# Attention weighing in half steps, values and identity products moved into the lead, and a later output store, in a two-layer transformer kernel on one core

## The reference

```python
x = norm(x + state_space(x))          # first layer: a scan, then a mixture of experts
x = norm(x + experts(x))              # top 2 of 8
x = norm(x + attention(x))            # second layer: 16 heads of 16 features
x = norm(x + ffn(x))                  # gate/up/down, inputs and weights rounded to FP4

def attention(z):                     # per sequence; this is where the change lies
    zn = norm(z) * ln_w + ln_b
    q, k, v = split(zn @ W_qkv + b_qkv)            # 16 heads of 16
    a = softmax(q @ k.T / 4)                       # 1024 x 1024 for each head
    return z + concat(a @ v) @ W_proj + b_proj
```

## Time and profile before

| | |
|---|---|
| median of 3 runs | 1861.14 us (1858.03 to 1862.63) |
| the profiled execution | 1861.33 us, span 1859.8 us |
| mean granted TensorE clock | 0.907 |
| PE busy | 1623.9 us (87%) |
| DVE busy | 1275.1 us (69%) |
| ACT busy | 829.0 us (45%) |
| POOL busy | 245.7 us (13%) |

### The profile page before, as it was taken

One profiled execution on the slowest core, in us unless ns is written; L12 is line 12 of the kernel. 1 busy time (PEld: TensorE's weight loads), 2 busy tenths in 40 slices (PEclk: granted clock), 3 DMA queues, 4 the chain that ended last, 5 costly groups with the idle time before them and its releaser, 6 DMA issues.

```text
span 1859.8 us, 25712 instructions
## 1 busy us (share of the span) xinstructions
PE 1623.9 (87%) x7834; PEld 926.9 (50%) x7834; DVE 1275.1 (69%) x2551; ACT 829.0 (45%) x1255; POOL 245.7 (13%) x243
## 2 busy tenths in 40 slices
PE   5969999993899996989999788899986988999786
PEld 2748888882433324654333356433334653333354
DVE  3672222202589977858999687779968958997586
ACT  1302332230357773242776624257772333777421
POOL 0243222213000302010012030100303010000020
PEclk8989999997779998995999989779998986999898
DMA  3227777673412300022231000412300031210000
GB/s 127 68 70 233 259 224 231 226 219 110 68 19 36 86 2 1 1 51 42 36 71 35 1 1 2 92 18 36 87 2 1 1 65 30 40 31 1 1 1 23
DMA packets 80185, 123.06 MB, mean 66 GB/s; under 512 B 13529, under 2 KB 55770, under 8 KB 80042
## 3 DMA queue, kind: packets, MB, share of 16 engines
q1 hardware_dynamic: 71050, 94.25, 19.5%
q0 software_dynamic: 8992, 27.01, 4.9%
HBM read 76.84 MB, written 18.61 MB: 51 GB/s over the span
## 4 chain that ended last, share of the span: by engine, by line
PE 69%; DVE 19%; issue 6%; ACT 3%; POOL 1%; DMA 1%; SPq 0%; DVEq 0%; ACTq 0%; POOLq 0%
PE PS L953 12%; PE PS L998 12%; DVE MX L1449 10%; PE PS L870 7%; PE PS L882 7%; PE PS L1082 7%; PE PS L1092 5%; PE PS L927 3%; PE PS L985 3%; PE PS L939 2%; PE PS L821 1%; ACT Pb L691 1%; PE PS L1043 1%; PE PS L1112 1%; PE PS L860 1%
## 5 line engine op out<-in xcount | busy, mean ns | idle before, releaser
L1449 DVE TENSOR_REDUCE MX<-PS 128x1 f32<-128x512 f32 x1024 | 635.3, 682 | 84.0 <-PE PS L953 84.0
L691 ACT ACTIVATE Pb<-PS 128x1024 f32<-128x1024 f32 x512 | 499.7, 1023 | 253.1 <-PE PS L985 252.1
L953 PE MATMUL PS<-Ks,Qs 48*128 48x512 f32 x1024 | 404.9, 502 | 36.6 <-DVE MX L1449 14.2
L953 PEld LDWEIGHTS PS<-Ks,Qs 48*128 48x128 f32 x1024 | 181.7, 203 | 370.7 <-DVE MX L1449 352.6
L985 PE MATMUL PS<-Qs,Ks 50*128 50x512 f32 x1024 | 311.2, 460 | 5.9 <-ACT Pb L691 4.7
L998 PE MATMUL PS<-Pb,V 128*32 128x512 f32 x2048 | 290.2, 640 | 2.7 <-ACT Pb L691 2.7
L985 PEld LDWEIGHTS PS<-Qs,Ks 50*128 50x128 f32 x1024 | 145.5, 198 | 57.4 <-ACT Pb L691 52.4
L1350 DVE TENSOR_TENSOR V<-PS,V 128x512 f32<-128x512 f32 x39 | 27.0, 692 | 203.3 <-PE PS L882 203.3
L882 PE MATMUL PS<-Pb,OT 128*128 128x256 f32 x624 | 141.0, 379 | 0.0
L614 ACT ACTIVATE OT<-PS,b1t 128x256 f32<-128x256 f32 x156 | 65.5, 471 | 158.9 <-PE PS L870 158.9
L882 PEld LDWEIGHTS PS<-Pb,OT 128*128 128x128 f32 x624 | 115.7, 190 | 14.2
(11 more groups left out here) (278 smaller groups left out, 1834.6 us busy)
## 6 DMA issues: line engine op xcount, KB each, us to landing
Pb<-W SPq DMA_DIRECT2D x78, 512.0 KB, 4.0
y_slot<-V SPq DMA_DIRECT2D x39, 256.0 KB, 4.0
Qs<-Qh SPq DMA_DIRECT2D x128, 64.0 KB, 2.3
Ks<-Kh SPq DMA_DIRECT2D x128, 64.0 KB, 2.3
V<-b SPq DMA_DIRECT2D x39, 128.0 KB, 3.7
XT<-x_mid POOLq DMA_DIRECT2D x4, 1024.0 KB, 6.2
out<-X POOLq DMA_DIRECT2D x4, 1024.0 KB, 6.6
OT<-xT SPq DMA_DIRECT2D x2, 1024.0 KB, 6.4
```

What stands on the lines that cost most here:

```text
L691: F["ex"].inc(act.activation(Pb[:, kt % 2, 2 * qh:2 * qh + 2, :], PS[:, 2 * qh:2 * qh + 2, :], ACT.Exp, scale=0.25))
L953: F["slp"].inc(pe.matmul(PS[:, slot_bank(i), :], Qs[rows, p % NB, t * P:(t + 1) * P], Ks[rows, p % NB, kh * HALF:(kh + 1) * HALF], start=T ...
L1449: F["sld"].inc(dve.tensor_reduce(MX[:, p % 2, a, t, kh:kh + 1], PS[:, slot_bank(i), :], AX.X, ALU.max))
```

## The change

It has these parts:

1. **Weighing in halves.** W is split by query halves. Half qh waits only for the exponentials of half qh and writes 256 columns of bank 7 in each column group. The order of query tiles in the stack changes to match. A step is now S, T, S, W twice. `pv` counts halves, and ScalarE waits for the half it overwrites. The copy of bank 7 comes after the first exponential of a pair's first step, not after the second.
2. **Values and identity products in the lead.** `EARLY` is 2. Three S follow, then for each further value up to five S. `keep_warm` adds products of the identity with itself, whose result nobody reads: 8 after the first pair's last S, 3 after the next S, and one after each of the next five.
3. **Late last turn.** The turn of pair 7's maxima moves from right behind the last S to step 53, after its second T.
4. **Output in its own buffer.** The last norm writes `OB` (a part of `Pb`). Pool copies the next residual into `X` when the FFN's last sum is done, and stores `OB` once the first stack has landed. It sets the ones of `V` after that store.
5. **Stack of K shared with Pool.** Three of the twelve DMAs of the first stack (keys of head 1) are issued by Pool.
6. **Loop edge.** The rounding of QK unit 2 (ScalarE) and the low parts of units 0 and 1 (VectorE) move ahead of the loop edge.

```diff
@@ SP: stack(p) @@
-                        for a in range(2):
+                        for a in range(1 if p == 0 and dst is Ks else 2):
@@ Pool @@
-            def sequence(b, more):
-                F["xw"].wait(pool, b, TT)
+            def residual(b, ahead):
+                F["xw"].wait(pool, b, TT, ahead)
                 hold(pool, "pool")
                 F["xn"].inc(pool.tensor_copy(X[:, :, :], XN))
-                F["xn"].wait(pool, b, 1)
+            def first_keys(b, ahead):
+                F["qkv"].wait(pool, b, 4, ahead)
+                hold(pool, "pool")
+                for row, part in enumerate((Kh[DH:2 * DH, 0, :].bitcast(F32), Kh[DH:2 * DH, 0, :].bitcast(F32), Kl[0][DH:2 * DH, :].bitcast(F32))):
+                    at = ROW + row * DH
+                    F["kst"].inc(pool.dma_start(Ks[at:at + DH, 0, :].bitcast(F32), part), by=16)
+            def value_ones(b, ahead):
+                F["xn"].wait(pool, b, 1, ahead)
                 hold(pool, "pool")
                 F["vm"].inc(pool.memset(V[:, :, :, DH:32], 1.0))
...
+                if more:
+                    F["dr"].wait(pool, b, TT)
+                    residual(b, 1)
+                    first_keys(b, 1)
+                    F["stk0"].wait(pool, b, STK - KST, 1)
                 F["xa"].wait(pool, b, TT - 2 + TT // 2)
                 F["xd"].wait(pool, b, 2 + TT // 2)
-                F["outd"].inc(pool.dma_start(out..., X[:, :, :]), by=16)
+                F["outd"].inc(pool.dma_start(out..., OB), by=16)
                 F["outd"].wait(pool, b, 16)
+                if more:
+                    value_ones(b, 1)
@@ ScalarE @@
-                    F["pv"].wait(act, b, KT * (p + 1))
+                    F["pv"].wait(act, b, 2 * KT * (p + 1))
...
-                                F["pv"].wait(act, b, (n - 4) // 2 + 1)
+                                F["pv"].wait(act, b, n - 3)
...
-                        if kt == 0 and p > 0:
-                            evac_o(p - 1)
+                            if kt == 0 and p > 0 and qh == 0:
+                                evac_o(p - 1)
@@ TensorE @@
-                    for a in range(2):
+                    for a in (1, 0):
...
-                def weigh(m):
+                def weigh(m, qh):
                     p, kt = m // KT, m % KT
                     if kt == 0 and p:
                         F["ov"].wait(pe, b, p)
-                    F["ex"].wait(pe, b, 2 * m + 2)
-                    for qh in range(2):
+                    F["ex"].wait(pe, b, 2 * m + qh + 1)
+                    for c in range(2):
                         for a in range(2):
-                            j = 2 * a + qh
-                            ins = pe.matmul(PS[32 * j:32 * j + 32, 7, :], V[:, kt, 2 * p + a, :], Pb[:, kt % 2, 2 * qh + a, :],
-                                            start=(kt == 0), stop=(kt == KT - 1), skip_group_check=True)
+                            j = 2 * a + c
+                            ins = pe.matmul(PS[32 * j:32 * j + 32, 7, qh * QW:(qh + 1) * QW], V[:, kt, 2 * p + a, :],
+                                            Pb[:, kt % 2, 2 * qh + a, c * QW:(c + 1) * QW],
+                                            start=(kt == 0 and qh == 0), stop=(kt == KT - 1), skip_group_check=True)
                     F["pv"].inc(ins)
+                def keep_warm(n):
+                    for _ in range(n):
+                        pe.matmul(PS[:, 3, 0:P], ident[:, :], ident[:, :], start=True, stop=True)

                 for t in range(EARLY):
                     values(t)
-                F["vv"].wait(pe, b, EARLY - 1)
+                F["vv"].wait(pe, b, 1)
+                maxima(3)
                 F["qkv"].wait(pe, b, 8)
                 for t in range(EARLY, TT):
-                    maxima(8 * (t - EARLY + 1))
+                    maxima(5 * (t - EARLY + 1))
                     values(t)
                 F["vv"].wait(pe, b, TT)
                 F["vm"].wait(pe, b, 1)
-                maxima(UN + START)
+                maxima(UN)
+                keep_warm(8)
+                maxima(UN + SOON)
+                keep_warm(3)
+                for n in range(SOON, START):
+                    maxima(UN + n + 1)
+                    keep_warm(1)
+                LAST = (NP * UN - UN - LEAD) // 4
...
-                    transposed_scores(p, kt, 0)
-                    maxima(ahead + 2)
-                    transposed_scores(p, kt, 1)
-                    maxima(ahead + 3)
-                    if m:
-                        weigh(m - 1)
-                    maxima(ahead + step)
-                weigh(NP * KT - 1)
+                    for qh in range(2):
+                        maxima(ahead + 2 * qh + 1)
+                        transposed_scores(p, kt, qh)
+                        if qh and m == LAST:
+                            turn_max(NP - 1)
+                        maxima(ahead + (step if qh else 2))
+                        if m:
+                            weigh(m - 1, qh)
+                for qh in range(2):
+                    weigh(NP * KT - 1, qh)
```

More of the change, by code:

```diff
@@ L20 @@
 HALF = 512
+QW = HALF // 2
 NH = S // HALF
@@ L32 @@
 LEAD, START = 12, 6
-EARLY = 5
+EARLY = 2
 SOON, LATER = 1, 4
@@ L225, in transformer @@
         XQ = Pf[0]
+        OB = XQ.rearrange("p (t d) -> p t d", t=TT)
         XW = Pf[1][:, TT * D // 2:]
@@ L262, in transformer @@
             ve=1, rs=2, nm=1, vel=2, rsl=4, nml=2, zn=TT, xn=1, xw=TT, xa=TT - 2 + TT // 2, xd=2 + TT // 2, x2=1, vm=1, trp=4 + 2, xt=4 + 2, xl=TT - 3,
-            qkp=8, qka=8, qkv=8, vp=TT, vv=TT, **{f"stk{k}": NP // NB * STK for k in range(NB)}, mrow=16 * 2 * NP,
+            qkp=8, qka=8, qkv=8, vp=TT, vv=TT, **{f"stk{k}": NP // NB * STK - (0 if k else KST) for k in range(NB)}, kst=KST, mrow=16 * 2 * NP,
             slp=SLOTS, sld=SLOTS, nms=NP,
-            bp=2 * KT * NP, ex=2 * KT * NP, pv=KT * NP, ov=NP,
+            bp=2 * KT * NP, ex=2 * KT * NP, pv=2 * KT * NP, ov=NP,
             op=TT // 2, on=TT, mp=TT, mt=TT, pr=TT, rr=TT,
@@ L548, in _ @@
             gathers(range(TT // 2))
+            residual(0, 0)
+            first_keys(0, 0)
+            value_ones(0, 0)
             with pool.Fori(0, B - 1) as b:
@@ L755, in sequence @@
                 late_rows(1, (6, 7))
+                if more:
+                    qk_evac(b, 1, (2,))
             ahead_root(0, 0)
@@ L947, in score_max @@
                     if r == 0:
-                        F[f"stk{p % NB}"].wait(pe, b, (p // NB + 1) * STK)
+                        F[f"stk{p % NB}"].wait(pe, b, (p // NB + 1) * STK - (0 if p % NB else KST))
+                    if n == 0:
+                        F["kst"].wait(pe, b, KST)
                     i = unit_slot(n)
@@ L1401, in ahead_norm, with qk_low @@
                                                      rstd[:, :, :], ALU.mult, ALU.mult))
+            def qk_low(b, ahead, units):
+                for u in units:
+                    c, w, th = u // 4, (u % 4) // 2, u % 2
+                    F["qka"].wait(dve, b, u + 1, ahead)
+                    hi, lo = ((Kh, Kl) if w else (Qh, Ql))
+                    sl = slice(th * HALF, (th + 1) * HALF)
+                    F["qkv"].inc(dve.scalar_tensor_tensor(lo[c][:, sl], PS[:, u % 4, :], bqkv[:, w * DC + c:w * DC + c + 1],
+                                                          hi[:, c, sl].bitcast(F32), ALU.add, ALU.subtract))
+                    F["qkv"].wait(dve, b, u + 1, ahead)
             def sequence(b, more):
@@ L1431, in late_norm @@
                     for t in range(own):
-                        F["xd"].inc(dve.tensor_scalar(X[:, t, :], R2[:, t, :], mvl[:, t, 0:1], rl[:, t:t + 1],
+                        F["xd"].inc(dve.tensor_scalar((OB if i else X)[:, t, :], R2[:, t, :], mvl[:, t, 0:1], rl[:, t:t + 1],
                                                       ALU.subtract, ALU.mult))
-                for u in range(8):
-                    c, w, th = u // 4, (u % 4) // 2, u % 2
-                    F["qka"].wait(dve, b, u + 1)
-                    hi, lo = ((Kh, Kl) if w else (Qh, Ql))
-                    sl = slice(th * HALF, (th + 1) * HALF)
-                    F["qkv"].inc(dve.scalar_tensor_tensor(lo[c][:, sl], PS[:, u % 4, :], bqkv[:, w * DC + c:w * DC + c + 1],
-                                                          hi[:, c, sl].bitcast(F32), ALU.add, ALU.subtract))
-                    F["qkv"].wait(dve, b, u + 1)
+                qk_low(b, 0, range(2, 8))
                 def row_maxima(lo, hi):
@@ L1568, in sequence @@
                 late_norm(1, late_statistics("dr", TT - 1), TT // 2)
+                if more:
+                    qk_low(b, 1, (0, 1))
                 assert links[0] == CHAIN, links
```

23 lines of the change are left out of this document (12 added, 11 removed).

## The result

The changed kernel takes 1851.76 us (median of 20 runs, 1843.17 to 1872.61), the kernel before 1861.04 us (20 runs, 1855.74 to 1866.55) on the same chip. The ratio is 0.9949, with a 95% interval of 0.9928 to 0.9971. The kernel is 0.5% faster, where 5.3% was forecast; 1762 us and the whole range to 1808 were missed. The profiled execution took 1852.25 us.

The account below looks back on a forecast made before the run. TensorE and VectorE were taken to stop each other in turn, partly at 1.2 GHz, leaving VectorE idle 78.8 us in the T loops. T loops 69, lead 13 and tail 17 made 99 us: 1861 to 1762 us; forecast 1747 to 1782 (0.60), range 1745 to 1808.

Parts of the forecast that it names:

- T loops: From first transposed-score product (T) to last row maximum (R) of each sequence: 69 us less, VectorE nearly always busy.
- leads: From first row maximum to first transposed-score product: 24.3 us becomes 23.7 a sequence, 2.4 us less in all.
- first R sooner: Before the lead: first S, and so first row maximum, comes three value products earlier, 2.6 us a sequence, 10.4 in all.
- tails: Last row maximum to last copy of weighed values: at ScalarE's pace, 22.0 us a sequence for 26.3, saving 17 us.
- the 85 us (17.9 steps at 4.76): T loop time at 1.2 GHz: with full clock through the lead, its steps take 3.0 us, 31 of the 78.8 us.
- the first rival: Clock falls in the lead anyway, identity products delay the turn some 2 us a sequence: 1804 us, chance 0.15.
- The rival of a T loop at 1.2 GHz: Slower: the T loop itself runs at 1.2 GHz, 3.8 us a step; 1930 us at 120 such steps, chance 0.04.
- late at pair starts: Rival at pair starts in the T loop: maximum rows come late, 28 times 1 us gives 1790 us, chance 0.09.
- the rival in which TensorE stays the limit: T loop: half a W costs 0.85 us, not 0.56, so the step stays 2.70 us: 1810 us, chance 0.12.
- set 10 aside: T loop: 2.5 us a sequence left as VectorE waiting, 0.5 at the start, the rest at pair ends.
- The term of 78.8 us: T loops: VectorE's idle time, 629.1 us less 550.3 of work, all of which would go if it never waited.
- the lower end, by columns: Lead: an identity product takes 0.22 us of 0.22 to 0.43, eight 1.7 of 1.7 to 3.5, adding nothing.

Follow-up runs that it names:

- its last repeat: The changed kernel run again unchanged on slower chips, as reference for two variants: 1913.41 us, ratio 1.0 to the kernel before.
- halves alone: Kernel before with only weighing in halves, order S T S W twice and new query tile order; old lead and last turn: ratios 1.0392 and 1.0422.
- the best version: The changed kernel with whole weighing in the first ten steps of each T loop and no identity products: 1884.87 us, 0.9863 of the kernel before.

## Why the prediction was wrong

| stage, four sequences | before | forecast | measured |
|---|---|---|---|
| T loops | 629.1 | 560.1 | 624.6 |
| leads | 97.2 | 94.8 | 114.7 |
| first R sooner | | -10.4 | -11.9 |
| tails | 105.2 | 88 | 94.2 |

Against the forecast the T loops are 64.5 us longer, the leads 19.9 and the tails 6.2.

**The step that failed** is "I expect full clock through the lead, so that the 85 us (17.9 steps at 4.76) go". Two things were wrong in it. First, the clock fell all the same, 17 us behind the first R in every sequence, when TensorE waited 0.65 us for ScalarE's copy of the last value. In two sequences it was back 3.4 us later and fell again 4 us behind the first T. That was the first rival, and one of its two halves was named rightly, but sized too small: identity products at 1.2 GHz hold up the turn. I gave 2 us a sequence for it; it was 7.3 in two sequences and 2.7 in two. Second, and larger, that rival still took the 17.9 low steps of before. That rests on an assumption that I never stated: that the new steps bring the clock back as soon as the old ones did. Weighing in one piece, the first stretch ended at most 27 us behind the first T in all 24 sequences profiled (before, and five experiments). In interleaved halves it ended 33 to 75 us behind it in 23 of 24, and in one it never began. Three of these six profiles are of executions near their kernel's median (the changed kernel, its last repeat, halves alone), and they show the same in 12 of 12. The changed kernel has 145 us at 1.2 GHz, in which VectorE does 152 reductions; at the forecast's 0.605 us each, and 0.7 for each of the four pair ends in them, they would be 95 us. So, by this estimate, 50 of the 64.5 us that the T loops missed lie there. The rival of a T loop at 1.2 GHz had the mechanism's other half, but put at 0.04 and without the lead's part in it.

The Trainium skill, "TensorE: Matmul & The Clock Gate", Part 1, says that activity releases the throttle. Here TensorE was busy for 14.00 of 14.00 us in windows that stayed low with either weighing, so by the records' busy share the rule gives no time for the return; the form of the work has to be looked at too.

**Right.** Half a W took 0.57 us (0.56 forecast, 1.01 at 1.2 GHz). The first R came sooner: 11.9 us for 10.4. Pool's share of the stack, its memset and the late store cost nothing that shows. The maximum rows weren't late at pair starts (the first step of a pair takes 2.48 us as the others), so that rival didn't come.

**Sizes.** A pair of S and T takes 0.335 us, not 0.25, so TensorE's half step is 1.24 and not 1.06, just above VectorE's 1.21. That is the rival in which TensorE stays the limit, narrowly and by another term than half a W. Over some 180 steps at full clock it is 11 us. The wait for the copy of bank 7 and the two steps round a turn (3.17 and 2.75 us) cost 1.4 us in each pair, where VectorE's own work between pairs is 0.7; that is some 15 us more. I had set 10 aside; with the 50 at 1.2 GHz these estimates make 66 of the 64.5 us. The term of 78.8 us was too large as well: the 550.3 us of work in it are those of the row maxima alone, and with the other instructions VectorE was busy 559.9 of 629.1 us, idle 69. The T pair and half W show in the tail too: I let ScalarE set its pace at 0.945 us, and it was TensorE's, 1.00. That is 1.2 us over 22 half steps, and the copy in step 57 adds 0.7; a tail took 23.6 and not 22.0 us, 94.2 in all. The late turn did what it was put there for: no wait, clock 1.0. Identity products: "I take the lower end, by columns, and so nothing on the path". At full clock that was right (in the third lead the instructions of the three behind S 32 start 0.11 us apart, so 0.22 a product). At 1.2 GHz eight took 3.8 us, above even the upper end of 3.5, since that was taken at full clock.

**Open.** What in a dense weighing the clock responds to isn't settled. The experiments exclude the matmul's length and the order of S and T; both variants look equally busy. The one run with whole weighing in every step and the new lead had the old last turn, and the best version didn't run on the first chip.

## What to carry to other kernels

A finer interleaving that fills TensorE at full clock can be the worse one at half clock: price a reordering at both clocks, and ask for each stretch that starts low what ends it, since "busy" doesn't. Work added to hold the clock costs double just when it fails; put it where nothing waits behind it, or leave it out, as here. And edits can lean on each other: halves without the late last turn and the new lead cost 4%, over half of it in the tails.

## What the runs showed of the hardware

**The slower chips stall beside the gathers.** On them the first three T loops of every kernel are longer than the last, mostly by 20 to 35 us (173.8, 173.5, 173.7 and 150.7 in the best version); on the first chip they aren't. Windows in the second T loop of the best version, while Pool gathers the next sequence's input, then one of the changed kernel on the first chip at the same work:

```profile
978.00:982.00 4.00, 4.00 (x44) 1.37 (x37) 3.90 (x9) 3.36 (x4) 2.92 (x5) 1.00 0.65 181
982.00:986.00 4.00, 2.79 (x20) 1.02 (x16) 2.73 (x5) 1.44 (x2) 2.85 (x4) 1.00 0.67 216
986.00:990.00 4.00, 1.76 (x11) 0.43 (x10) 0.28 (x1) 0.28 (x1) 3.09 (x4) 0.52 0.33 98
994.00:998.00 4.00, 1.22 (x3) 0.50 (x3) 0.69 (x1) 0.23 (x1) 3.09 (x4) 0.50 0.37 108
1002.00:1006.00 4.00, 2.91 (x17) 1.01 (x17) 2.83 (x5) 1.94 (x2) 0.00 (x0) 0.50 0.00 0
```
```profile
985.00:990.00 5.00, 4.95 (x50) 1.80 (x46) 4.65 (x9) 3.96 (x6) 3.78 (x5) 1.00 0.39 105
```

From 984 to 1002 three engines stand idle for much of the time, while Pool issues its gathers at their usual 0.95 us; they go on when the gathers end, with the clock low for 12 us more. VectorE's timeline names no engine of this core as the releaser:

```profile
1002.35 2.48 DVE L1516 TENSOR_REDUCE MX<-PS 128x1 f32<-128x512 f32 x4 [7.06 <-remote]
```

The waits begin before the clock falls (at 986.1), so here the low clock follows a stall and isn't its cause. What the engines wait for isn't shown.

**The clock falls with TensorE nearly busy.** In the lead of the changed kernel one wait of 0.65 us precedes the fall, after 4 us in which TensorE was busy for 3.26. In the third sequence it was back at 1.0 at the first T, with TensorE then busy for 3.72 of 4 us, and fell again 4 us on for 31 us:

```profile
1200.00:1204.00 4.00, 3.72 (x23) 1.64 (x21) 3.84 (x7) 2.63 (x3) 0.00 (x0) 1.00 0.00 0
1204.50:1234.60 30.10, 30.10 (x162) 10.46 (x160) 20.86 (x36) 13.06 (x13) 0.00 (x0) 0.50 0.00 1
```

The spread of the changed kernel (1843 to 1873 us) goes with the clock: its mean over an execution goes from 0.911 in the shortest to 0.889 in one of the longest. In which stretch they differ isn't shown, since one was profiled.
